# The fourth attention's first norms and projections inside the linear mixture's tiles, and the slot weights' transfers spread

## The reference, cut to what matters

```python
x = x + tanh(g_xattn[0]) * L0_xattn(ctx, layernorm(x), mask)   # 4 heads
x = x + tanh(g_ffn[0])   * L0_ffn(layernorm(x))                # one of 8 gated experts
x = x + tanh(g_xattn[1]) * L1_xattn(layernorm(x), ctx)         # 8 heads
x = x + tanh(g_ffn[1])   * L1_ffn(layernorm(x))                # squared ReLU experts
x = x + tanh(g_xattn[2]) * L2_xattn(layernorm(x), ctx)         # 4 heads
x = x + tanh(g_ffn[2])   * L2_ffn(layernorm(x))                # the linear mixture
x = x + tanh(g_xattn[3]) * L3_xattn(layernorm(x), ctx)         # the fourth attention, one head
x = x + tanh(g_ffn[3])   * L3_ffn(layernorm(x))                # the slot mixer

def L2_ffn(x):                       # linear mixture: 8 experts, each one 256 x 256 matrix
    w = one-hot top 2 of (x @ gate_w.T), softmax over the two
    return sum_e w[e] * (x @ weight[e])

def L3_xattn(x, ctx):
    x1, x2 = layernorm(x) * ln1_g + ln1_b, layernorm(ctx) * ln2_g + ln2_b
    q, k, v = x1 @ Wq + bq, x2 @ Wk + bk, x2 @ Wv + bv
    return softmax(q @ k.T / 16) @ v @ Wo + bo
```

## Time and profile before

| | us |
|---|---|
| median of 3 runs | 1883.88 |
| lowest and highest | 1882.06, 1885.59 |
| the profiled execution | 1889.61 |
| its span from first to last instruction | 1887.8 |
| TensorE busy in it | 1638.3 (87%) |
| VectorE busy | 955.4 (51%) |
| mean granted TensorE clock | 0.926 |

### The profile page before, as it was taken

The page is one execution under the profiler, slowest core; times in us unless marked ns, Lnnn a source line. Parts: engine busy times, 40 slices in busy tenths (PEclk is TensorE's granted clock), DMA queues, the critical chain, the costliest instruction groups (busy, mean ns, idle before and its releaser), DMA issues.

```text
span 1887.8 us, 30379 instructions
## 1 busy us (share of the span) xinstructions
PE 1638.3 (87%) x9090; PEld 1160.8 (61%) x9090; DVE 955.4 (51%) x3005; ACT 634.2 (34%) x1796; POOL 300.2 (16%) x394
## 2 busy tenths in 40 slices
PE   6899899729999899999999899799979958887776
PEld 2555555529999766666666666567755436665454
DVE  4788787422222244444443346354546546765553
ACT  3555555212332233333333242233320014442321
POOL 4545445030000300000000001000000111112000
PEclk9999999659999899999999699899988979996887
DMA  4000008059999300000000000100000030000001
GB/s 104 14 15 16 20 14 238 1 184 323 327 321 324 109 18 12 7 12 12 12 12 1 1 12 20 30 23 24 18 6 9 20 123 28 26 18 1 1 1 35
DMA packets 88417, 117.36 MB, mean 62 GB/s; under 512 B 16428, under 2 KB 80140, under 8 KB 83212
## 3 DMA queue, kind: packets, MB, share of 16 engines
q1 hardware_dynamic: 85228, 113.05, 18.8%
q0 software_dynamic: 2048, 3.29, 0.6%
q10 hardware_dynamic: 1056, 0.01, 0.0%
HBM read 104.51 MB, written 8.52 MB: 60 GB/s over the span
## 4 chain that ended last, share of the span: by engine, by line
PE 68%; issue 13%; DVE 7%; ACT 5%; DMA 3%; POOL 3%; SPq 0%; DVEq 0%; ACTq 0%; POOLq 0%
PE bank L2064 14%; PE bank L2177 7%; PE bank L2345 6%; PE bank L2150 5%; PE bank L2446 5%; PE bank L2123 4%; PE bank L2161 4%; PE bank L2207 3%; PE bank L2359 3%; PE bank L2401 3%; PE bank L2115 3%; PE bank L2417 2%; PE bank L2533 2%; DMA work<-in_F_b1c 2%; DVE work L1393 1%
## 5 line engine op out<-in xcount | busy, mean ns | idle before, releaser
L953 ACT ACTIVATE work<-bank,work 100x361 f32<-100x361 f32 (+1 forms) x272 | 158.7, 590 | 251.5 <-DVE work L1393 227.1
L2177 PEld LDWEIGHTS bank<-work 128*100 128x100 f32 x1760 | 186.8, 172 | 57.0 <-issue 29.8
L1402 DVE COPY work<-bank 128x300 f32<-128x300 f32 (+1 forms) x272 | 123.0, 489 | 184.6 <-PE bank L2161 184.0
L2177 PE MATMUL bank<-work 128*100 128x64 f32 (+1 forms) x1760 | 191.0, 260 | 12.4 <-DVE work L1402 12.4
L2345 PE MATMUL bank<-work 128*128 128x128 f32 x1280 | 151.7, 277 | 1.5 <-DMA work<-in_F_b1c 0.9
L2345 PEld LDWEIGHTS bank<-work 128*128 128x128 f32 x1280 | 149.1, 193 | 3.6 <-ACT work L1086 1.8
L1699 DVE SCALAR_TENSOR_TENSOR work<-bank,work 128x128 f32<-128x128 f32 x160 | 56.1, 350 | 180.7 <-PE bank L2345 168.1
L1393 DVE TENSOR_REDUCE work<-bank 100x1 f32<-100x361 f32 x208 | 101.9, 528 | 76.4 <-PE bank L2150 62.4
L751 POOL TENSOR_TENSOR work<-work,neg_half 100x1 f32<-100x1 f32 x96 | 53.2, 554 | 540.1 <-DVE work L1349 540.0
L2150 PE MATMUL bank<-work 64*100 64x361 f32 (+1 forms) x512 | 120.8, 549 | 1.1 <-ACT work L938 0.6
L2161 PE MATMUL bank<-ident,work 100*128 100x100 f32 x880 | 104.5, 254 | 7.3 <-ACT work L953 6.3
(11 more groups left out here) (294 smaller groups left out, 2805.4 us busy)
## 6 DMA issues: line engine op xcount, KB each, us to landing
work<-in_F_w SPq DMA_DIRECT2D x60, 1024.0 KB, 5.5
work<-in_ctxT SPq DMA_DIRECT2D x64, 135.4 KB, 2.2
work<-in_ctx SPq DMA_DIRECT2D x32, 192.0 KB, 2.5
sorted_x<-zeros SPq DMA_DIRECT2D x1, 2560.0 KB, 10.4
work<-in_F_b SPq DMA_DIRECT2D x20, 128.0 KB, 6.9
work<-sorted_x SPq DMA_DIRECT2D x20, 128.0 KB, 3.0
sorted_y<-work SPq DMA_DIRECT2D x20, 128.0 KB, 5.8
work<-in_ctx SPq DMA_DIRECT2D x32, 78.8 KB, 2.4
```

Source lines behind the costliest of these rows:

```text
L953: nc.scalar.activation(pr[:, 0:NK], S_bank[k][0:T, 0:NK], ACT.Exp, bias=nmax[k][0:T, :], accum_out=rsum[j][0:T, h:h + 1]).then_inc(s.exped ...
L1402: nc.vector.tensor_copy(PT[k][:, 0:CH, :], PT_bank[k][:, 0:CH * T].rearrange("p (c t) -> p c t", c=CH)).then_inc(s.probs_copied.sem, 1)
L2177: ins = nc.tensor.matmul(to, PT[k][:, c, :], values, start=(c == 0), stop=(c == CH - 1))
```

## The change

The fourth attention no longer begins with a barrier, and the linear mixture is called from inside `attention(3)` of each engine.

- *Memory.* The mixtures' buffers move from the front of `work` to behind `unused_by_3`, so that they no longer lie on the fourth attention's. `Fmv` and `Frs` get a place of their own. The squared mixture's `HS` becomes nine separate buffers, five of them at the front.
- *VectorE.* `clear` runs behind tile 0's accumulates; the norms of batches 0 and 1 (without the context's normalising of batch 1) go in pieces behind tiles 4 to 10 (`while_weighing`). `ln_x` with k = 0 gets a wait until the mixture's addition of that batch is done, and a no-operation (`apart`) behind it.
- *GpSimd.* The powers of those norms go between the additions of batches 3 to 8 (`while_adding`).
- *TensorE.* Steps 0 to 3 of batch 0 go ahead of and between the last tile's four expert pairs, step 4 behind them (`first_step`); then TensorE waits until all pairs are combined. The steps of batch 0 write to the scores' banks (`step_bank`).
- *ScalarE.* Runs its part of the mixture first and then the copies of the steps.
- *SyncE.* Waits for the clearing, issues the contexts of batches 0 and 1, moves the tiles' rows, issues batch 2's context after tile 8, waits for phase 5's end, and then issues each further context with two of the 24 slot transfers behind it, in code without a loop.

```diff
+                def while_weighing(i):
+                    if i == 0:
+                        clear()
+                    if i == 4:
+                        ln_ctx_stats(0, 0)
+                    if i == 5:
+                        ln_x(0, 0, 0)
+                    if i == 6:
+                        ln_ctx_norm(0, 0)
+                        ln_x_norm(0, 0, 0)
+                        ln_x(0, 0, 1)
+                    if i == 7:
+                        ln_x_norm(0, 0, 1)
+                        ln_ctx_stats(1, 1)
+                    if i == 8:
+                        ln_x(1, 1, 0)
+                    if i == 9:
+                        ln_x_norm(1, 1, 0)
+                        ln_x(1, 1, 1)
+                    if i == 10:
+                        ln_x_norm(1, 1, 1)
...
                     if k:
                         wait_for(dve, s.ln_x, b)
+                    elif L == 3:
+                        wait_count(dve, mx2.resid, t + 1)
+                        apart(dve)
...
+                def while_adding(b):
+                    if b == 3:
+                        ctx_norm(0, 0)
+                    if b in (4, 5):
+                        x_norm(0, 0, b - 4)
+                    if b == 6:
+                        ctx_norm(1, 1)
+                    if b in (7, 8):
+                        x_norm(1, 1, b - 7)
...
                 for i in range(1, TILES):
+                    if i == TILES - 1:
+                        first_step(0)
                     for g in range(4):
                         experts(i, g)
+                        if i == TILES - 1:
+                            first_step(g + 1)
+                pe.wait_ge(s.combined, E2 * TILES)
                 end(pe)
...
                 if L == 3:
-                    load_slot_weights()
+                    linear_experts(lambda i: load(2, 0) if i == 8 else None)
+                    begin(sp, 6)
+                    for t in range(3, B):
+                        load(t, t % 2)
+                        load_slot_weights(2 * (t - 3), 2 * (t - 2) if t < B - 1 else len(slot_loads))
+                    return
```

More of the change, by code:

```diff
@@ L393, in flamingo_kernel @@
         area = Area()
[L394 to L405, removed]
         TXI = area.take(TILES0, dt=I32)
@@ L436, in flamingo_kernel @@
         RX = KT[0][:, 4 * P * PAIRS[0]:4 * P * PAIRS[0] + D]
-        area.at = normed
+        Fmv, Frs = area.take(B, 2), area.take(B)
+        area.at = unused_by_3
         GX = [area.take(D) for _ in range(4)]
@@ L445, in flamingo_kernel @@
         RL = [area.take(GROUP) for _ in range(2)]
-        HS = area.take(1 + E1, NTOK)
-        area.at = mixture
+        HS = [area.take(NTOK) for _ in range(4)]
+        area.at = 0
+        HS += [area.take(NTOK) for _ in range(1 + E1 - 4)]
+        assert area.at <= unused_by_3
+        area.at = 0
         XS = area.take(B, D + 1)
@@ L516, in vv0, with step_bank @@
             return V[q % 2][:, 1024 * (q // 2):1024 * (q // 2 + 1)].rearrange("p (c n) -> p c n", n=256)
+        def step_bank(L, t, j, n):
+            if L == 3 and isinstance(t, int) and t == 0:
+                return S_bank[n % 2]
+            return J_bank[(j * STEPS[L] + place_of(L, t, n)) % 2]
         def begin(eng, p):
@@ L706, in _ @@
                     attention(p // 2)
-                else:
-                    (routed_experts, squared_experts, linear_experts, slot_mixer)[p // 2]()
+                elif p != 5:
+                    (routed_experts, squared_experts, None, slot_mixer)[p // 2]()
             begin(sp, PHASES)
@@ L776, in attention @@
                     rows_back(1)
-                norms(0, 0)
-                norms(1, 1)
+                if L == 3:
+                    linear_experts(while_adding)
+                else:
+                    norms(0, 0)
+                    norms(1, 1)
                 if L == 1:
@@ L1291, in attention @@
                 H, W, NK, CH = HEADS[L], HWID[L], KEYS[L], CHUNKS[L]
-                if L != 1:
+                if L in (0, 2):
                     begin(dve, 2 * L)
[L1295 to L1311, removed]
@@ L1312, in attention, with clear @@
-                dve.drain().then_inc(s.cleared.sem, 1)
-                wait_for(dve, s.cleared, 1)
-                if L > 0:
+                def clear():
+                    for j in range(2):
+                        if L in (0, 3):
+                            nc.vector.memset(C[j][96:P, NCH - 1, :], 0.0)
+                        if L == 0:
+                            nc.vector.memset(XT[j][:, :, T:P], 0.0)
+                            nc.vector.memset(QK[j][96:P, 4, :], 1.0)
+                            if j == 0:
+                                nc.vector.memset(QKsq[96:P, 4, :], 1.0)
+                            nc.vector.memset(MR[j][0:T, NCH - 1, LAST:P], FAR)
+                            nc.vector.memset(MR[j][0:T, NCH, 0:T], 0.0)
+                            nc.vector.memset(MR[j][0:T, NCH, T:P], FAR)
+                        if L == 2:
+                            nc.vector.memset(CT[j][:, :, NC:NKP], 0.0)
+                        if L == 3:
+                            nc.vector.memset(CT[j][CW[1]:CW[1] + 1, 1, :], 1.0)
+                        if L > 0:
+                            nc.vector.memset(PR[j][0:T, NCH - 1, LAST:P], 0.0)
+                    dve.drain().then_inc(s.cleared.sem, 1)
+                    wait_for(dve, s.cleared, 1)
@@ L1315, in attention @@
+                if L < 3:
+                    clear()
+                if L in (1, 2):
                     dve.wait_ge(loaded[2 * L], 16 * n_loads[2 * L])
@@ L2211, in project, with first_step @@
                     ins.then_inc(s.out.sem, 1)
+                def first_step(n):
+                    if n == 0:
+                        wait_for(pe, s.cleared, 1)
+                        pe.wait_ge(loaded[6], 16 * n_loads[6])
+                    step(0, 0, n)
                 def prepare(t, j):
+                    if L == 3:
+                        linear_experts(first_step)
+                        return
                     for n in steps_of(L, t):
```

76 lines of the change are left out of this document (46 added, 30 removed).

## The result

The changed kernel takes 1869.87 us (median of 4 runs, 1868.23 to 1872.44) beside 1884.74 for the kernel before: ratio 0.9922, 95% interval 0.9901 to 0.9942, so a gain of 11 to 19 us where 20.3 was forecast. The time lies inside the stated range, at its upper edge, but the forecast gain lies outside of what this comparison allows. The experiments ask where the difference sits: in the steps of the sum, or outside of them.

What follows compares the result with a forecast made beforehand. The prediction saw the seam before the fourth attention as the weak place and VectorE's chain as setting 9.65 us a batch. 18.0 + 4.7 + 1.2 - 2.2 - 1.4 = 20.3 us gained, giving 1863.6; range 1858.5 to 1870.

Steps and rivals of the forecast that it cites:

- Reading of the seam: Between linear mixture and fourth attention: the weak place, TensorE idle 14.75 us before its first transpose, first scores at 1545.56.
- (a): Last tile: batch 0's first steps go between and behind the experts, first scores at about 1527.6 instead of 1545.56, gain 18.0.
- (e): VectorE's chain, batches 2 to 15: new wait for the addition with its no-operation costs 0.10 each, loss 1.4, bounds 0 to 3.5.
- (b): Tiles 4 to 10: norms of batches 0 and 1 fit into VectorE's idle time there and cost nothing.
- The slower rival: In the tiles: VectorE's added pieces stall TensorE by the banks and its clock falls, 1887.6 us; chance 0.05.
- (c): First two attention batches: earlier context loads and spread slot weights bring both to the steady 9.65, gains 4.7 and 1.2.
- (d): TensorE's clock falls once near the end of the new first batch, loss 2.2, from 0 to 4.4.
- (f): Moved buffers and the squared mixture's split of HS change addresses only and cost nothing.

Runs made afterwards that it cites:

- first steps behind the experts: Changed kernel with the five first steps behind the last tile's experts instead of between them: 1867.93 us, ratio 0.9901.
- The fill: Changed kernel with two products of 512 columns, results unused, in TensorE's first-batch wait for the context norm: 1863.91 us, ratio 0.9876.
- late addition: Changed kernel with GpSimd's last addition held until VectorE has normalised batch 1's context: 1861.69 us, ratio 0.9874.
- one wait: Changed kernel with the addition waits of batches 3 to 15 replaced by one wait for all 16 in batch 2: 1859.87 us, ratio 0.9860.
- no no-operation: Changed kernel with the waits for the additions in every batch but without the no-operation behind each: 1860.56 us, ratio 0.9870.
- slot weights at once: Changed kernel with the 24 slot weight transfers issued at once, ahead of batch 3's context: 1877.42 us, ratio 0.9952.
- barrier kept: Changed kernel with the barrier at the fourth attention's start kept on TensorE and VectorE: 1865.78 us, ratio 0.9897.
- both with the idle products: Changed kernel with two unused first-batch products, alone (1863.91 us) or together with one wait for all additions and GpSimd's last addition held back (1860.81 us).
- the repeats: Both kernels timed again without edits: changed kernel 1865.88 us, ratio 0.9884; kernel before 1885.19 and 1884.29 us.
- the ten comparisons above: The changed kernel's two and its eight edits' comparisons with the kernel before: median time gain less stretch gain between -5.2 and +5.8 us, mean +1.0.

## Why the prediction was right or wrong

- **Reading of the seam: right, the closeness of the sum in part luck.** Stretch 20.1 less, forecast 20.3. Against its forecast (a) gained 0.5 less, the first batch 0.6 less and the second 1.0 more, and (e) cost 0.2 more; these nearly cancel.
- **(a) 18.0, measured 17.5.** First logits to first scores went from 105.2 + 22.3 = 127.5 us to 108.0 + 2.0 = 110.0. The four steps cost 2.8 us between the experts (108.0 - 105.2), not 2.27. From the start of each step to the next expert product it is 2.27 in sum, as forecast; but from a group's first product to the step behind it are 1.86 us in the last tile (1518.22 to 1520.08), where a group took 1.72. But the reason given for their place, that round trips to ScalarE hide there, is worth under 1 us, as the first steps behind the experts showed.
- **(b) Right.** The tiles that got the pieces of work follow one another at 6.87 us as before. TensorE's expert products stayed at 592 ns, and it was busy 20 of 20 us from 1460 to 1480, while VectorE's work there rose from 11.4 to 13.2 (kernel before, then the changed one). The slower rival is refuted with it.

```profile
1460.00:1480.00 20.00, 20.00 (x48) 8.93 (x47) 11.39 (x24) 0.00 (x0) 2.33 (x4) 1.00 0.06 19
```
```profile
1460.00:1480.00 20.00, 20.00 (x48) 8.93 (x47) 13.19 (x34) 0.00 (x0) 4.09 (x6) 1.00 0.06 17
L2523 PE MATMUL bank<-F_weight,work x208: 592/592/1223, 1423.1 to 1527.1; 128*128 128x512 f32 x96, 128*64 128x512 f32 x8
```

- **(c) 4.7 and 1.2.** Together with (d): the first batch fell from 14.37 to 11.27 (forecast 9.65 + 0.98 = 10.63), the second from 10.86 to 9.88 (forecast 10.86). GpSimd was in time: it ended its last addition at 1531.84, and served batch 2's norm at 1534.03. What the step missed is that the addition, in time or not, now lay on top of VectorE's context norm: 1.47 us instead of 0.95. That is 0.5 of the 0.6 us by which the first batch came out longer than forecast.
- **(d) Right in kind, 1.3 instead of 2.2.** The clock fell at 1534, in the middle of the first batch and not near its end, and was back at about 1541, before most of the second batch. The fill removed it, so TensorE's waiting is the cause. What decides is open. From the first scores on, five us each, for the changed kernel (it fell at the end of them), the steps behind the experts (it stayed up) and the late addition (it fell at their end):

```profile
1529.05:1534.05 5.00, 2.82 (x16) 1.90 (x16) 3.29 (x12) 2.12 (x6) 0.93 (x2) 1.00 0.09 20
```
```profile
1532.17:1537.17 5.00, 3.35 (x20) 2.42 (x21) 3.19 (x13) 2.53 (x6) 0.55 (x1) 1.00 0.15 40
```
```profile
1521.65:1526.73 5.08, 3.43 (x21) 2.50 (x22) 3.24 (x14) 2.53 (x6) 1.36 (x2) 1.00 0.06 13
```

The last two are alike, TensorE busy 3.4 us in each, and they end differently. By the 2 us windows of one profiled execution each, it fell in seven kernels with this seam (both of the change, one wait, no no-operation, late addition, slot weights at once, barrier kept) and stayed up in three (both with the idle products, and the steps behind the experts). The Trainium skill's sentence weighed in the prediction, that a copy by VectorE does not cool TensorE (TensorE: Matmul & The Clock Gate, "Loop structure matters more than you think"), is not put to the test at the seam: the clock fell at 1534, before that copy (1537.77), behind a wait of 2.00 us for VectorE's context norm. The steady loop agrees with it, with such a copy in every batch and the granted clock at 1.00.
- **(e) Right: 12 steady batches x 0.13 = 1.6,** forecast 1.4.
- **(f) Right for the whole time;** whether the moved buffers lengthen the routed stage is open.
- **The step that failed is the last, from the sum to the time.** The prediction took 20.3 us off the profiled execution, which gave 1869.3, and then 5.7 more, because the median of three runs lay that far below the profiled one; around it stood 1.5 us of scatter. The changed kernel's profiled execution took 1870.73, only 1.4 off, but it lay 0.86 above its median, not 5.7. In the repeats the same difference was 5.8 above (changed kernel) and 1.0 below (kernel before): it is scatter and no property of the kernel. And scatter is larger than the 1.5: twelve runs of one kernel lay within 12.6 us, and the 14 profiles put it in stages in which the change reorders nothing. The first comparison showed 14.9 us for a change whose stretch gains 20.1, and the second 21.5 (1887.39 - 1865.88). That the missing 5 us of the first is such scatter fits the ten comparisons above and its own profile (outside part 1610.6, near the top of 1600.0 to 1611.4), but only one of its four runs has a profile that I could split; this remains likely, not shown.

## What to carry to other kernels

Price an edit in the shortest stretch of the trace that holds all of it, and compare that stretch; whole times of this kernel scatter by more than most of these edits are worth. Where a chain of one engine sets a loop's period, count every wait and no-operation that is put in it, and put one wait for the last event ahead of the loop if it is met by then. And ask of a load not only when it is issued but what lies ahead of it in the queue, and what work there is to lie over its delay.

## What the runs showed of the hardware

- GpSimd's addition of two SBUF inputs (0.72 us) and VectorE's `tensor_scalar` of one SBUF input (0.37 us) hold each other up: side by side they took 0.91 and up to 0.89 us, in all six traces in which they met, and 0.77 at most and 0.38 with the late addition, the steps behind the experts and the barrier kept, in which they didn't. The kernel before never showed it (378 ns at most in all 96). In the changed kernel both were over 1.03 us after the first began, where one behind the other they would take 0.72 + 0.37 = 1.09: hardly anything is won by the overlap. The Trainium skill (SBUF — State Buffer, "Who interferes with whom") says that the two engines share one pair of ports, that `tensor_scalar` may be among the instructions that take it, and that whoever is second waits for the whole instruction. The trace agrees that one of them is held; that the first too became longer is more than it says.
- A met wait with a register sum cost 0.08 us in VectorE's chain, a no-operation 0.05 (starts 0.12, 0.20 and 0.25 apart).
- A context's load issued behind the 24 slot transfers was used 8.1 us after its issue (slot weights at once) and 7.7 (kernel before), where the median of such loads lands after 2.5: some 5 us more.
- TensorE kept its upper clock level through windows at 0.94, 1.63 and 0.71 busy of 2 us (steps behind the experts); in the changed kernel it lost it behind two at 0.69 and 1.14. With the same busy time of 3.4 us from the first scores on it kept it once and lost it once, so busy time alone did not decide.
